# Fewer spent waits on TensorE in the second and third tile of a tiled recommender interaction

## The chip, the cores and the metric

The kernel runs on 1 core of one Trainium2 chip. The metric is the device time in microseconds (us). The kernel before was timed three times: 610.24, 610.33 and 610.54 us, median 610.33 us. In what follows an engine is named by its part in the profile: PE is TensorE's matrix product, PEld its loading of weights, DVE is VectorE, ACT is ScalarE, SP is SyncE.

## The reference, cut to what matters

```python
B, NF, D = 2048, 64, 128                    # r_F is (B, NF, D), all in float32
Kf  = einsum('bjd,ed->bje', F, K_w)         # keys: one 128x128 product per row of F
S   = einsum('bid,bjd->bij', F, Kf)         # a 64x64 score matrix per sample
out = einsum('bij,ijd->bid', S, W)          # each score row i times its own 64x128 matrix
out = out + einsum('bid,ed->bie', F, Q_w)   # plus a second 128x128 product of F
```

## The kernel before

The 2048 samples are cut into 16 tiles of 128 samples (`TILES`). A tile is 8 units of 16 samples, or 16 chunks of 512 columns (a chunk is 8 samples with their 64 features). For each tile TensorE runs three stages, called P, S and R here, with the tile's number behind:

- **P** (`project`, from line 472): for each of 16 chunks the product with the key matrix and the product with the query matrix. Each is done to nearly full float32 precision in three passes (`three`, line 446): high part by high part, high by low, low by high. That is 6 matrix instructions of 512 columns a chunk and 96 in a tile. ScalarE copies both results out of PSUM; ScalarE and VectorE split the coming units of F into a high and a low part.
- **S** (`scores`, line 500): 128 small float32 products, one for each sample; the profile has two records of 64 columns for each, so 256 in a tile. ScalarE and VectorE copy the scores to `s_t`.
- **R** (`rows_tile`, line 547): for every feature a product of 64 scores with its own matrix of W; 64 instructions, 128 records. VectorE adds the query part (`sum_out`, line 363) and SP stores 512 KB after each of 8 row blocks.

The order on TensorE is written out by hand at line 577: P0, then for each tile t: S(t), P(t+1), R(t). In the last tile two of the 16 query products are kept back and stand between S15 and R15 (`LATE = 2`, line 38), so P15 has 90 matrix instructions.

Every engine has its own list of instructions and waits on semaphores for the others. In `project` TensorE waits for the low half of the unit (`flo_done`, line 484), and for the PSUM bank it is about to write (`kf_copied`, line 487; `s_copied`, line 490; `q_copied`, line 493). Behind each chunk's two products the loop at lines 497 and 498 puts a number of waits on `zeros_done`. That semaphore is raised once, at the start of the kernel, so such a wait is always met: it is a spent wait, which does nothing but stand in TensorE's list of instructions. `FILL` (lines 41 to 43) says how many stand in a tile, spread evenly over the 16 chunks: 466 in tile 1, 108 in each of tiles 2 to 14, 128 in tile 15, none in tile 0. These are 1998 in all.

In the instructions that come of this, a wait that stands right ahead of a weight load rides on that load, and the others are packed two to one instruction. The profile shows them as event-semaphore instructions at the line of their first wait. By my count of the code a tile from 2 to 14 is 960 weight loads and matrix products and 64 such instructions, together 1024. P1 has 243 of them and a P of tiles 2 to 14 has 61, with the products' own waits and those behind the last chunk.

F comes in pairs of units, 1 MB each, into a ring of six places (`f_ring`). The first are loaded by SP at the start, with W (2 MB) behind them (line 181). The later ones are issued by ScalarE in `load_next` (line 244), one at the start of each P and one after its chunks 3, 7 and 11.

Of the kernel before, what the change touches and what calls it, by code (L numbers as in the profile page):

```python
# [14 lines left out]
TILES = B // P  # L15
# [22 lines left out]
LATE = 2  # L38


FILL = {1: 466}
FILL.update((t, 108) for t in range(2, TILES - 1))
FILL[TILES - 1] = 128

BOTH = [v for v in range(FIRST, TILES * UNITS) if v in (4, 5) or v >= UNITS and v % UNITS in (0, 4, 6)]

# [1 line left out]
def build(nc, first, f_0, f_t, w, out):  # L48
    with ExitStack() as ctx:  # L49
# [395 lines left out]
        def _(pe):  # L445
# [26 lines left out]
            def project(t):  # L472

                for c in range(CHUNKS):
# [21 lines left out]
                    if t >= 1:  # L496
                        for x in range(FILL[t] * c // CHUNKS, FILL[t] * (c + 1) // CHUNKS):
                            pe.wait_ge(zeros_done, 1)
# [110 lines left out]
```

## Time and profile before

| | |
|---|---|
| median of three runs | 610.33 us |
| the profiled execution | 610.46 us |
| its span, first to last instruction | 608.7 us |
| PE busy, share of the span | 599.6 us, 99% |
| ACT and DVE busy | 402.3 and 399.2 us, 66% each |
| DMA, mean over the span | 227 GB/s |

The span is the profiled execution without 1.8 us around it. A busy share is an average over stages of different kinds; the stages P, S and R have to be read by themselves. The profile's times are counted from the start of the span. A matrix product's record is longer than the distance to the next one, since the products overlap; distances between starts, and lengths of whole stages, are what time is made of.

### The profile page before, as it was taken

Reading aid. Unit: us, or ns where it says so; the run is one execution under the profiler, and the core shown is the slowest. Engines: PE = TensorE matmul, PEld = TensorE weight load, DVE = VectorE, ACT = ScalarE, POOL = GpSimd, SP = SyncE. Lnnn points to the kernel's source line nnn. Section 1 sums busy time; section 2 is a strip of 40 time slices with the busy share of each in tenths; the row PEclk is TensorE's granted clock in tenths of the full one; section 3 lists DMA queues with packets and bytes.
Section 4 is the critical chain, followed back from the end, with each engine's and each line's share of the span. In section 5 each row is a group of like instructions: output and inputs, shape, how many; then the busy total and the mean of one; then the engine's idle time right before and its main releaser. Section 6 shows DMA issues by size and latency. Waiting matters only on the chain.

```text
span 608.7 us, 18157 instructions
## 1 busy us (share of the span) xinstructions
PE 599.6 (99%) x7690; PEld 525.4 (86%) x7690; DVE 399.2 (66%) x412; ACT 402.3 (66%) x696; POOL 0.2 (0%) x4
## 2 busy tenths in 40 slices
PE   9999999999999999999999999999999999999995
PEld 7876988889898898988989888898988989889895
DVE  5644947658575676856759476585756768567386
ACT  7878295692938849386592956929488393865921
POOL 0000000000000000000000000000000000000000
PEclk9999999999999999999999999999999999999999
DMA  8633755647576485755657556475654857457177
GB/s 335 261 141 139 279 208 214 245 167 295 191 268 219 166 321 178 285 172 213 264 207 280 208 209 248 169 295 191 265 222 163 324 175 286 174 210 267 69 279 277
DMA packets 29453, 138.14 MB, mean 227 GB/s; under 512 B 3264, under 2 KB 3776, under 8 KB 21312
## 3 DMA queue, kind: packets, MB, share of 16 engines
q1 hardware_dynamic: 20736, 75.83, 31.6%
q10 hardware_dynamic: 8640, 61.15, 28.5%
q8 instruction: 64, 1.05, 0.7%
q14 instruction: 13, 0.11, 0.0%
HBM read 69.86 MB, written 67.11 MB: 225 GB/s over the span
## 4 chain that ended last, share of the span: by engine, by line
PE 97%; DVE 1%; issue 1%; DVEq 0%
PE ps L447 20%; PE ps L509 20%; PE ps L449 19%; PE ps L448 19%; PE ps L541 18%; DVE o_sb L372 1%; PE ps L576 1%; DVEq L49 0%; DVE o_sb L382 0%; PE ps L467 0%; PE ps L465 0%; PE ps L469 0%; DVE f_hi L388 0%; DVEq L115 0%
## 5 line engine op out<-in xcount | busy, mean ns | idle before, releaser
L337 DVE TENSOR_TENSOR f_lo<-f_ring,f_hi 128x1024 fp32r<-128x1024 f32 x124 | 151.8, 1224 | 169.5 <-ACT f_hi L217 167.9
L231 ACT ACTIVATE q_out<-ps 128x512 f32<-128x512 f32 x256 | 157.2, 614 | 6.9
L222 ACT ACTIVATE kf<-ps 128x512 f32<-128x512 f32 x256 | 155.9, 609 | 6.0 <-PE ps L449 2.2
L372 DVE TENSOR_TENSOR o_sb<-ps,q_out 128x1024 f32<-128x1024 f32 x127 | 145.1, 1214 | 20.1 <-PE ps L541 20.1
L240 ACT ACTIVATE s_t<-ps 128x512 f32<-128x512 f32 x32 | 19.1, 598 | 176.1 <-PE ps L509 176.1
L509 PE MATMUL ps<-f_ring,kf 128*64 128x64 f32 x4096 | 123.3, 222 | 0.3 <-issue 0.3
L509 PEld LDWEIGHTS ps<-f_ring,kf 128*64 128x64 f32 x4096 | 121.0, 138 | 2.6 <-issue 0.8
L541 PEld LDWEIGHTS ps<-s_t,w_sb 64*128 64x128 f32 x2048 | 115.6, 188 | 5.8 <-issue 5.8
L541 PE MATMUL ps<-s_t,w_sb 64*128 64x128 f32 x2048 | 118.6, 274 | 0.1
L447 PE MATMUL ps<-f_hi,k_hi 128*128 128x512 f32 x255 | 102.1, 400 | 0.6
L447 PE MATMUL ps<-f_hi,q_hi 128*128 128x512 f32 x256 | 99.9, 390 | 0.0
L449 PE MATMUL ps<-f_hi,q_lo 128*128 128x512 f32 x256 | 99.7, 390 | 0.0
L448 PE MATMUL ps<-f_lo,q_hi 128*128 128x512 f32 x256 | 99.6, 389 | 0.0
L449 PE MATMUL ps<-f_hi,k_lo 128*128 128x512 f32 x255 | 99.5, 390 | 0.0
L448 PE MATMUL ps<-f_lo,k_hi 128*128 128x512 f32 x255 | 99.4, 390 | 0.0
L217 ACT ACTIVATE f_hi<-f_ring 128x1024 fp32r<-128x1024 f32 x77 | 82.0, 1065 | 0.0
L447 PEld LDWEIGHTS ps<-f_hi,k_hi 128*128 128x128 f32 x255 | 47.8, 188 | 16.1 <-issue 6.0
L447 PEld LDWEIGHTS ps<-f_hi,q_hi 128*128 128x128 f32 x256 | 48.2, 188 | 10.2 <-ACT s_t L242 0.2
L448 PEld LDWEIGHTS ps<-f_lo,q_hi 128*128 128x128 f32 x256 | 48.1, 188 | 10.2
L449 PEld LDWEIGHTS ps<-f_hi,q_lo 128*128 128x128 f32 x256 | 48.0, 188 | 10.2
L449 PEld LDWEIGHTS ps<-f_hi,k_lo 128*128 128x128 f32 x255 | 47.9, 188 | 10.2
L448 PEld LDWEIGHTS ps<-f_lo,k_hi 128*128 128x128 f32 x255 | 47.9, 188 | 8.8
(39 smaller groups left out, 161.2 us busy)
## 6 DMA issues: line engine op xcount, KB each, us to landing
out<-o_sb SPq DMA_DIRECT2D x127, 512.0 KB, 3.4
f_ring<-f_t ACTq DMA_DIRECT2D x58, 1024.0 KB, 4.7
f_ring<-f_t SPq DMA_DIRECT2D x4, 1024.0 KB, 10.9
f_ring<-f SPq DMA_DIRECT2D x8, 256.0 KB, 5.7
w_sb<-w SPq DMA_DIRECT2D x1, 2048.0 KB, 18.2
out<-o_sb SPq DMA_DIRECT2D x2, 256.0 KB, 2.7
o_sb<-first SPq DMA_DIRECT2D x1, 192.0 KB, 2.9
o_sb<-first ACTq DMA_DIRECT2D x1, 192.0 KB, 3.4
```

The source lines that it names most:

```text
L217: nc.scalar.activation(f_hi[:, v % SPLIT, :], f_unit(v), COPY).then_inc(fhi_done, 1)
L222: nc.scalar.activation(kf[:, c // 2, c % 2 * CK:(c % 2 + 1) * CK, :, :].rearrange("d k h i -> d (k h i)"), ps[:, 2 * c % 8, :], COPY).then ...
L231: nc.scalar.activation(q_out[:, t % 2, :, :].rearrange("d i (h b) -> d i h b", h=2)[:, :, :, at:at + CK], q_bank(t * CHUNKS + c).rearrange ...
L240: nc.scalar.activation(s_t[:, :, same], src[:, 0, :, :], COPY)
L337: nc.vector.tensor_tensor(f_lo[:, v % SPLIT, :], f_unit(v), f_hi[:, v % SPLIT, :].bitcast(F32), ALU.subtract).then_inc(flo_done, 1)
L372: nc.vector.tensor_tensor(o_sb[:, n % OBUF, :, :, :].rearrange("d x s b -> d s x b"), ps[:, bank:bank + 2, :].rearrange("d s (x b) -> d s ...
L447: nc.tensor.matmul(dst, w_hi[:, :], hi, start=True, stop=False)
L448: nc.tensor.matmul(dst, w_hi[:, :], lo, start=False, stop=False)
L449: return nc.tensor.matmul(dst, w_lo[:, :], hi, start=False, stop=True)
L509: ins = nc.tensor.matmul(ps[h * N:(h + 1) * N, e, k * N:(k + 1) * N], kf[:, e, k, h, :], rows, start=True, stop=True)
L541: ins = nc.tensor.matmul(ps[:, at + s, col:col + P], w_sb[half, m, :], cols, start=True, stop=True)
L576: nc.tensor.matmul(ps[:, 0, :], zeros, zeros.unsqueeze(1).broadcast_to([D, BANK // P, P]), start=True, stop=True)
```

## The change

Three numbers: tile 1 gets no spent waits in place of 466, tile 2 gets 56 in place of 108, tile 15 gets 132 in place of 128. Tiles 3 to 14 keep 108. There are 1484 in all.

```diff
-FILL = {1: 466}
-FILL.update((t, 108) for t in range(2, TILES - 1))
-FILL[TILES - 1] = 128
+FILL = {1: 0, 2: 56}
+FILL.update((t, 108) for t in range(3, TILES - 1))
+FILL[TILES - 1] = 132
```

## Rows read from the trace of the kernel before

**Rows 1.** The page: busy time, share of the span, instructions.

```profile
span 608.7 us, 18157 instructions
...
PE 599.6 (99%) x7690; PEld 525.4 (86%) x7690; DVE 399.2 (66%) x412; ACT 402.3 (66%) x696; POOL 0.2 (0%) x4
```

**Rows 2.** The page: the chain that ended last, by engine.

```profile
PE 97%; DVE 1%; issue 1%; DVEq 0%
```

**Rows 3.** Table by stage: P1, P2, P3, P4, P15; window, length, busy, clock, DMA share, GB/s.

```profile
34.61:60.84 26.23, 25.50 (x100) 16.88 (x97) 10.98 (x11) 22.75 (x39) 0.00 (x0) 1.00 0.45 161
...
75.80:97.80 22.00, 22.00 (x100) 17.94 (x97) 10.99 (x11) 21.27 (x38) 0.00 (x0) 1.00 0.54 192
...
112.86:134.86 22.00, 22.00 (x100) 17.94 (x96) 10.90 (x11) 21.27 (x38) 0.00 (x0) 1.00 0.53 193
...
149.82:171.83 22.01, 22.01 (x101) 17.94 (x97) 11.00 (x11) 21.27 (x38) 0.00 (x0) 1.00 0.55 192
...
556.45:577.10 20.65, 20.65 (x94) 16.81 (x91) 8.06 (x8) 19.82 (x35) 0.00 (x0) 1.00 0.29 103
```

**Rows 4.** Line 498, spent waits alone: P1; 1.3 us within P1; P2.

```profile
L498 PEldq EVENT_SEMAPHORE  x212: 51/51/51, 34.6 to 60.4; - x106
...
L498 PEldq EVENT_SEMAPHORE  x12: 51/51/51, 35.7 to 36.9; - x12
...
L498 PEldq EVENT_SEMAPHORE  x32: 51/51/51, 76.8 to 93.8; - x32
```

**Rows 5.** Timeline of the weight loads, P1, around a chunk's start.

```profile
37.01 0.19 PEld L449 LDWEIGHTS ps<-f_hi,q_lo 128*128 128x128 f32 x1
37.38 0.19 PEld L447 LDWEIGHTS ps<-f_hi,k_hi 128*128 128x128 f32 x1 [0.18 <-issue]
```

**Rows 6.** Timeline of DVE: first splits of P1, then the same of P2.

```profile
39.59 1.22 DVE L337 TENSOR_TENSOR f_lo<-f_ring,f_hi 128x1024 fp32r<-128x1024 f32 x1 [4.63 <-ACT f_hi L217]
...
80.79 1.22 DVE L337 TENSOR_TENSOR f_lo<-f_ring,f_hi 128x1024 fp32r<-128x1024 f32 x1 [4.35 <-ACT f_hi L217]
```

**Rows 7.** Timeline of ACT's queue: loads of F in P1, then in P2.

```profile
34.74 0.33 ACTq L249 DMA_DIRECT2D f_ring<-f_t  x1
...
40.73 0.33 ACTq L249 DMA_DIRECT2D f_ring<-f_t  x1
...
75.93 0.33 ACTq L249 DMA_DIRECT2D f_ring<-f_t  x1
...
81.60 0.33 ACTq L249 DMA_DIRECT2D f_ring<-f_t  x1
```

**Rows 8.** SP's issue of W's load, and the page's time to landing.

```profile
7.98 0.43 SPq L181 DMA_DIRECT2D w_sb<-w  x1
```

```profile
w_sb<-w SPq DMA_DIRECT2D x1, 2048.0 KB, 18.2
```

**Rows 9.** Table by stage: S0, S1, S2, S4, S14, S15, and after S15.

```profile
26.99:34.61 7.62, 7.62 (x257) 7.55 (x257) 5.12 (x8) 3.61 (x6) 0.00 (x0) 1.00 0.02 4
...
68.18:75.80 7.62, 7.62 (x258) 7.55 (x257) 7.53 (x10) 1.78 (x3) 0.00 (x0) 1.00 0.88 339
...
105.14:112.86 7.72, 7.72 (x258) 7.63 (x257) 7.63 (x10) 1.78 (x3) 0.00 (x0) 1.00 0.86 332
...
142.21:149.82 7.61, 7.61 (x258) 7.54 (x256) 7.52 (x10) 1.78 (x3) 0.00 (x0) 1.00 0.87 339
...
548.84:556.45 7.61, 7.61 (x258) 7.54 (x256) 7.53 (x10) 1.78 (x3) 0.00 (x0) 1.00 0.87 336
...
584.44:592.71 8.27, 7.95 (x258) 7.67 (x256) 5.87 (x9) 3.56 (x6) 0.00 (x0) 1.00 0.80 312
592.71:608.67 15.96, 9.02 (x134) 8.27 (x134) 9.68 (x10) 2.25 (x5) 0.00 (x0) 0.93 0.67 264
```

**Rows 10.** Timeline of PE through S15: 147 records, a gap, 109 records.

```profile
584.45 4.53 PE L509 MATMUL ps<-f_ring,kf 128*64 128x64 f32 x147
589.27 3.42 PE L509 MATMUL ps<-f_ring,kf 128*64 128x64 f32 x109 [0.30 <-issue]
```

**Rows 11.** DMA queues: the whole span; 180.47 to 181.47 (S4); 586.75 to 587.75 (S15).

```profile
q8 instruction: 64, 1.05, 0.7%
...
q8 instruction: 1, 0.02, 8.0%
...
q8 instruction: 1, 0.02, 5.5%
```

## The prediction

> **What bounds the kernel now.** I read four views in this order. The page's busy times come first: PE is busy 99% of the span, and DVE and ACT 66% each [rows 1]. The chain of waits says the same from the other side: 97% of the chain that ended last is PE's own work [rows 2]. So time is won only where TensorE itself takes longer than its products need. The reader can't see that place in a busy share, since PE counts as busy nearly everywhere. It is seen in the third view, the table by stage [rows 3]. P2, P3 and P4 take 22.00, 22.00 and 22.01 us for 96 products, which is 0.2292 us each. P15, with 90 products, takes 20.65 us, or 0.2294 each. P1 has the same 96 products and takes 26.23 us. The clock granted is 1.00 in all five, so TensorE ran at the upper of its two levels and the clock does not explain the difference.
>
> What P1 has more of is the spent waits. The fourth view, the one of line 498, counts 212 wait instructions in P1 that hold nothing but spent waits, and 32 in P2 [rows 4]. Twelve of them in a row start between 35.7 and 36.9 us: 1.2 us over 11 steps, some 0.11 us each. With the products' own waits P1 has 243 wait instructions by the count of the code, P2 has 61.
>
> **Why 61 are free and 243 are not.** A chunk of P1 has six products and 243 / 16 = 15.2 wait instructions. The waits alone are about 15.2 x 0.11 = 1.7 us, and the six products need 6 x 0.2292 = 1.375 us. The measured chunk is 26.23 / 16 = 1.64 us. So in P1 the engine that hands out TensorE's instructions (the sequencer) is the bound: it spends its time on waits while the array runs dry, and the array gets the next chunk late. The weight load of each chunk's first product shows it, with 0.18 us of idle time put down to "issue" [rows 5]. In P2 a chunk has 3.8 wait instructions, some 0.4 us, which lie beside 1.375 us of products. That is the work which hides them, and it hides more of them the fewer there are.
>
> **The change part by part.**
>
> *Tile 1, 466 to 0.* 234 of P1's wait instructions go, 9 stay. The longest work left in a chunk is the six products. I take P2's length for P1: 26.23 - 22.00 = **-4.23 us**. The whole of it is on PE's chain, so it moves everything behind P1 forward.
>
> The question is what comes late next in a P1 that is 4.2 us shorter. VectorE: the first split of a new unit starts 39.59 - 34.61 = 4.98 us into P1, and 80.79 - 75.80 = 4.99 us into P2 [rows 6]. Both lie in the same place, so P1 can follow P2's schedule. ScalarE is busy 22.75 us in P1 and 21.27 us in P2 [rows 3]. This is tight (21.27 of 22.00), but P2 shows that it fits, with the same instructions. F: the first load is issued 0.13 us into both stages and the second 6.1 us into P1 and 5.8 us into P2 [rows 7]; it follows the chunks and will come earlier with them. W, which R0 waits for, was issued at 7.98 and landed 18.2 us later, at 26.2 us [rows 8]. R0 will begin at 60.84 - 4.23 = 56.6 us, so 30 us of cover stay. P1 has no stores beside it, which P2 does not have either (its stores end with S2's last part). The bounds for this part: nothing below 22.00 us is seen for 96 products, and if ScalarE's longer 22.75 us had to be fitted in, the stage would be 0.75 us longer. So -4.23 to -3.48, and I take -4.23 by the nearer row.
>
> *Tile 2, 108 to 56.* P2's wait instructions go from 61 to 41 by the count. All 61 were covered; taking 20 away gives 0. If the cover were gone, each would cost 0.11 us, so 20 of them would bring a gain of 2.2 us. But P2 has the same time per product as P15 with its 74 [rows 3], so the waits of P2 set nothing, and I leave this end out.
>
> *Tile 15, 128 to 132.* Four waits make one wait instruction more by the count, beside 1.375 us of products a chunk: 0 by itself.
>
> *Where the borders between instruction blocks come to lie.* The page shows 64 transfers of the instruction queue, 1.05 MB together, 16 KB each [rows 11]. TensorE's list is 16,550 instructions by the count, so one transfer is about 1.05 MB / 16,550 = 63 bytes times 256. Tiles 2 to 14 are 1024 instructions each, four blocks exactly, so the borders lie in the same places in each of them. S15 shows what one can cost: after 147 records PE stands, and the other 109 follow 0.3 us later by the records [rows 10]. The stage is 8.27 us instead of 7.61, a loss of 0.66. S2 is 7.72 us, a loss of 0.11; S1, S4 and S14 are 7.61 or 7.62, like S0 [rows 9]. In S4 the transfer lies 1.3 to 2.3 us into the stage, in S15 it lies 2.3 to 3.3 us into it [rows 11]. I read this as one block fetched late, because it stood behind the stores. The DMA engines are 80 to 88% busy in S1 to S15 [rows 9].
>
> The change takes 234 + 20 = 254 instructions out ahead of tile 3, two less than a block of 256. In rounds 3 to 14 each border thus lies 2 instructions earlier in its stage than now, which at S's pace (7.61 us / 512 instructions = 0.015 us) is 0.03 us. In S1 it lies 22 instructions earlier, 0.33 us: PE would reach the second border of S1 at about 4.07 us instead of 4.40. In S15 it lies 3 earlier. Bounds for all of it: from -0.77 (both present losses, 0.66 and 0.11, go) to +0.66 in each stage that is hit. I take 0, because 13 of the 15 stages with stores beside them lose nothing now (three of the 13 stand in [rows 9], and they are alike), and 0.03 us is little beside the 1 us by which the transfer was later in S15.
>
> **The sum.** 610.46 us in the profiled execution, less 4.23, is 606.23. That execution is 0.13 us over the median of the runs shown, 610.33, so a median run comes to **606.1 us**.
>
> A page of the Trainium skill speaks to the borders (Runtime: NRT & Kernel Launch, section Instruction fetch mechanics). It says that instructions come in 16 KiB blocks of 256, that the next is fetched while one runs, and that a crossing is mostly hidden. The trace agrees on the 16 KB and not on the hiding in S15. By that rule alone the borders would never cost and the sum would be the same less S15's and S2's losses, which is the second case below. Another page (Advanced Engine Details and Errata, section ISA Cache) gives that cache only two lines, so that a block must come within one block's running. That is the mechanism of the fourth case.
>
> **The rivals.**
>
> *The present losses vanish.* S15's border moves and the fetch falls better: 606.1 - 0.77 = **605.4**. For it: 13 of 15 stages are clean. Against: the median run is only 0.13 below the profiled one, so the runs without a profile seem to hold the loss too, and a border that moves 3 instructions changes little.
>
> *The unsettled rounds stall.* S1 has its border 0.33 us earlier and S2 is hit again: one or two stages at 0.66 each, 606.8 to **607.4**. For it: S2 already lost 0.11 with its present border. Against: S1 is the only stage with a real shift, and its fetch is asked for earlier too.
>
> *Slower: every round's second border in S is missed.* The block fetch has to fit between two borders of an S, 256 x 0.015 = 3.8 us, among stores. If the shift puts it behind one more store in each round, S1 to S14 lose up to 0.66 as S15 does now, 14 x 0.66 = 9.2, less S2's 0.11: 606.1 + 9.1 = **615.2**. It decides from 4.23 / 14 = 0.30 us lost in each round. For it: the fetch is late by only 1 us where it costs 0.66. Against: clean rounds with a shift of 0.03 us are expected to stay clean, since nothing else in them moves.
>
> *The waits are not what makes P1 long.* P1 is the first stage after the start; if its operands or ScalarE held it, nothing would be gained and the time stays at **610.3**. Against: the equal places of rows 6, and the idle time of rows 5, which is "issue" and no other engine.
>
> **How the numbers follow.** The forecast, 606.1, has 55%. Losses vanish: 20%. One or two new stalls: 17%. All rounds stall: 5%. No gain: 3%. What this kernel's measurement can tell from no change is about 0.2%, 1.2 us. The first three cases are all more than that below 610.33, so faster is 92%; no gain is same, 3%; and all rounds stalled is slower, 5%. The range takes the first case with P1's bound of 0.75 us, the second, and the third as far as one and a half stalls: 605.2 to 607.2. Left out are 8% for the last two cases and some of the third.
>
> **What would show it.** P1 would run from 34.6 to 56.6, 22.0 us long, and line 498 would have no instruction there; P1's weight loads would show no "issue" idle. P2 should stay at 22.00. The instruction queue should show 63 transfers instead of 64. S1 to S14 should be 7.61 to 7.62 each, with single ones up to 0.7 longer, and what lies behind S15 should stay at 15.96 us. The prediction is wrong if P1 stays over 22.8 us, or if most S stages are over 7.8 us, with a gap in PE's records after some 135 to 147 of the 256.

## The result, and the profile after

The changed kernel took 606.53 us (median of 6 runs, 605.90 to 607.51) against 610.29 us for the kernel before (6 runs, 609.90 to 610.54). The ratio is 0.994, with a 95% interval from 0.9929 to 0.9951. The forecast was 606.1 us, in a range of 605.2 to 607.2. The changed kernel's runs lie 1.6 us apart, where those of before lie 0.6 apart.

The profiled execution took 606.42 us with a span of 604.6. The table by stage is in the same columns as [rows 3] and [rows 9]. The stages are P1, P2, S2, S3, S6, S14, P15, S15 and what lies behind S15:

```profile
34.45:56.43 21.98, 21.98 (x100) 17.94 (x96) 10.69 (x11) 21.25 (x38) 0.00 (x0) 1.00 0.55 193
...
71.39:93.63 22.24, 22.24 (x100) 17.87 (x96) 11.00 (x11) 21.42 (x38) 0.00 (x0) 1.00 0.54 190
100.98:109.13 8.15, 7.88 (x258) 7.67 (x257) 7.84 (x10) 1.78 (x3) 0.00 (x0) 1.00 0.81 317
...
138.46:146.24 7.78, 7.78 (x258) 7.67 (x256) 7.69 (x10) 1.78 (x3) 0.00 (x0) 1.00 0.85 331
249.50:257.25 7.75, 7.75 (x258) 7.67 (x256) 7.66 (x10) 1.78 (x3) 0.00 (x0) 1.00 0.86 331
545.37:552.99 7.62, 7.62 (x259) 7.55 (x257) 7.53 (x10) 1.78 (x3) 0.00 (x0) 1.00 0.87 337
552.99:573.63 20.64, 20.64 (x94) 16.81 (x90) 8.06 (x8) 19.82 (x35) 0.00 (x0) 1.00 0.29 103
580.98:588.70 7.72, 7.68 (x258) 7.54 (x257) 5.87 (x9) 3.56 (x6) 0.00 (x0) 1.00 0.86 334
588.70:604.60 15.90, 9.02 (x134) 8.27 (x134) 9.67 (x10) 2.25 (x5) 0.00 (x0) 0.92 0.67 266
```

P1 is 21.98 us long in place of 26.23. ScalarE, which stood at 22.75 us there, is now at 21.25. No wait instruction of line 498 is left in P1; the first one in the span starts at 70.9 us:

```profile
L498 PEldq EVENT_SEMAPHORE  x498: 51/51/51, 70.9 to 570.9; - x166
```

The weight load that opens a chunk of P1 no longer has idle time before it (in [rows 5] it had 0.18 us), and the instruction queue has 63 transfers:

```profile
36.85 0.19 PEld L449 LDWEIGHTS ps<-f_hi,q_lo 128*128 128x128 f32 x1
37.08 0.19 PEld L447 LDWEIGHTS ps<-f_hi,k_hi 128*128 128x128 f32 x1
```

```profile
q8 instruction: 63, 1.03, 0.7%
```

So much is as forecast. The S stages are not all clean. A clean one takes 7.61 or 7.62 us; S2 took 8.15, S3 7.78 and S6 7.75. P2 took 22.24 us, with the extra time behind its 7th product. S1, whose border moved most, is clean:

```profile
63.78:71.39 7.61, 7.61 (x258) 7.54 (x256) 7.52 (x10) 1.78 (x3) 0.00 (x0) 1.00 0.88 341
```

S15, at 7.72 us, is clean too. PE's records in it show no gap. The 0.11 us over 7.61 stand at its end, where the weight load of the first kept-back query product waits for ScalarE's copy of the scores:

```profile
588.70 0.19 PEld L447 LDWEIGHTS ps<-f_hi,q_hi 128*128 128x128 f32 x1 [0.17 <-ACT s_t L242]
```

The kernel before has the same wait there:

```profile
592.71 0.19 PEld L447 LDWEIGHTS ps<-f_hi,q_hi 128*128 128x128 f32 x1 [0.16 <-ACT s_t L242]
```

So of the 0.66 us that [rows 9] show for S15 over a clean stage only 0.55 are the late block.

The timeline of PE through S2 shows the same picture as [rows 10], one record earlier, after 146:

```profile
100.98 4.53 PE L509 MATMUL ps<-f_ring,kf 128*64 128x64 f32 x146
105.78 3.42 PE L509 MATMUL ps<-f_ring,kf 128*64 128x64 f32 x110 [0.27 <-issue]
```

The account between the two spans (608.7 to 604.6, -4.1 us): S0 begins 0.16 earlier (26.83 for 26.99), P1 -4.25, P2 +0.24, the late blocks in S from 0.66 (S2 0.11, S15 0.55) to 0.85 (S2 0.54, S3 0.17, S6 0.14), +0.19, the end behind S15 -0.06. That is -4.04; the rest is rounding and a few hundredths in other P stages. The present loss of S15 went, and three new ones came.

### The profile page after: what moved, and what is told of

Read it like the earlier page. It is cut to its first block, busy times and chain, and to the rows that moved or that the text cites. A ratio compares the mean times of both kernels' runs of the same rounds, so it can differ in the third digit from the quotient of the medians.

```text
span 604.6 us, 17904 instructions
## 1 busy us (share of the span) xinstructions
PE 596.4 (99%) x7690; PEld 526.3 (87%) x7690; DVE 399.2 (66%) x412; ACT 401.5 (66%) x696; POOL 0.2 (0%) x4
## 4 chain that ended last, share of the span: by engine, by line
PE 98%; DVE 1%; issue 1%; DVEq 0%
PE ps L509 20%; PE ps L447 20%; PE ps L449 19%; PE ps L448 19%; PE ps L541 18%; DVE o_sb L372 1%; PE ps L576 1%; DVEq L49 0%; DVE o_sb L382 0%; PE ps L467 0%; PE ps L465 0%; PE ps L469 0%; DVE f_hi L388 0%; DVEq L115 0%
```

## The experiments

In all of them a place x means: the first border between two blocks of 256 instructions lies x instructions into S (and into P and R, where the tile is 1024 instructions), by the count of the code. The kernel before has x = 40 in S1 to S14 and 39 in S15. The changed kernel has 18 in S1, 38 in S2 to S14 and 36 in S15. The count rests on one shift, taken from the gap of [rows 10]; every gap that follows is a test of it. The loss shows at the second border, 256 instructions behind the first. By the formula a gap should stand after (256 + x) / 2 - 1 records of S, give or take one.

**Twice the waits of tile 1.** The kernel before with

```diff
-FILL = {1: 466}
+FILL = {1: 978}
```

> The kernel before with 978 spent waits in tile 1 in place of 466, 256 wait instructions more by the count, so every border behind P1 lies where it lay before. Theory A (sequencer bound, each wait instruction some 0.106 us): 256 x 0.106 = 27.1 us more, 637.4 us, P1 53.3 us. Rival B (P1 was long for another reason, such as operands that come late after the start): about 610.3 us, no more than 2 us above.

It took 638.09 us (638.02 to 638.18), ratio 1.045 (1.0436 to 1.0463). P1 and P2 by stage:

```profile
34.48:88.49 54.01, 26.00 (x101) 16.80 (x97) 11.01 (x11) 25.50 (x40) 0.00 (x0) 1.00 0.23 78
103.45:125.43 21.98, 21.98 (x101) 17.94 (x97) 10.99 (x11) 21.25 (x38) 0.00 (x0) 1.00 0.55 192
```

Line 498 alone has 468 instructions in P1 here, against 212 in [rows 4], so the 256 more that the count gave are there. P1 grew by 54.01 - 26.23 = 27.78 us for them: 0.1085 us each. That times 243 is 26.4 us, and the P1 of before is 26.23. So P1's length was set by the number of its wait instructions, and theory A stands.

**As many waits as before, spread over two tiles.**

```diff
-FILL = {1: 466}
-FILL.update((t, 108) for t in range(2, TILES - 1))
+FILL = {1: 233, 2: 341}
+FILL.update((t, 108) for t in range(3, TILES - 1))
```

> About as many wait instructions as before, spread over two tiles: 233 spent waits in tile 1, 341 in tile 2, the rest as before (the borders from S2 on lie 38 instructions into a stage, as in the changed kernel from S2 on). Theory A (waits are free below some 13 wait instructions a chunk, since 13 x 0.106 = 1.375 us of products): P1 22.0 us, P2 22.0 us, total about 606.5 us, plus up to 0.7 for S1, whose borders lie 157 instructions in. Rival B (every spent wait costs, or the number of instructions does): 610.3 us, as before.

It took 607.36 us (606.91 to 607.71), ratio 0.9946 (0.9934 to 0.9958). P1 and P2, and the instructions of line 498 in each:

```profile
34.40:56.39 21.99, 21.99 (x101) 17.95 (x97) 10.70 (x11) 21.25 (x38) 0.00 (x0) 1.00 0.54 192
71.82:93.81 21.99, 21.99 (x99) 17.95 (x97) 11.49 (x12) 21.26 (x38) 0.00 (x0) 1.00 0.55 192
```

```profile
L498 PEldq EVENT_SEMAPHORE  x95: 51/51/51, 34.4 to 52.9; - x95
...
L498 PEldq EVENT_SEMAPHORE  x150: 51/51/51, 71.8 to 91.0; - x150
```

P2 holds 150 instructions of pure spent waits and is as fast as P1 with 95 or the changed kernel's with none. As many waits as before cost nothing when spread thinly enough; only their density in P1 of before did. Rival B falls. The median lies 0.8 us over the changed kernel's: in the profile S1, with x = 157, took 8.09 us, with its gap after 206 records where the formula asks for it, and S15 took 8.31.

**The part for tile 1 alone.** Tiles 2 and 15 keep 108 and 128; x is then 18 in every round.

```diff
-FILL = {1: 466}
+FILL = {1: 0}
```

> The part for tile 1 alone: 466 to 0, tile 2 keeps 108, tile 15 keeps 128. Theory A (P1 was bound by the handing out of its waits; a border's place matters): P1 is 22.0 us as in the changed kernel, but the borders now stay 18 instructions into every stage, where P2 of the changed kernel lost 0.24 us. If each of P2 to P15 loses 0.24, the time is 606.5 + 13 x 0.24 = 609.6 us. Rival B (the place of the borders does not matter, only the waits of tile 1 do): 606.5 us, as the whole change. Between 607.3 and 608.8 neither holds as stated.

It took 614.16 us (609.90 to 616.27, 12 runs), ratio 1.0048 (1.003 to 1.0067): half a per cent slower than the kernel before. Both theories missed, A by its price and its place. P1 has its 22 us, but the S stages have lost more than P1 won. S1, P2, S2, S5 and S9 by stage:

```profile
64.07:72.53 8.46, 7.83 (x258) 7.67 (x256) 7.83 (x10) 1.78 (x3) 0.00 (x0) 1.00 0.79 306
72.53:94.52 21.99, 21.99 (x99) 17.94 (x96) 10.69 (x11) 21.26 (x38) 0.00 (x0) 1.00 0.54 192
101.87:110.35 8.48, 7.83 (x259) 7.68 (x257) 7.84 (x10) 1.78 (x3) 0.00 (x0) 1.00 0.78 304
215.35:223.83 8.48, 7.83 (x259) 7.67 (x257) 7.84 (x10) 1.78 (x3) 0.00 (x0) 1.00 0.78 304
...
365.41:373.02 7.61, 7.61 (x258) 7.54 (x257) 7.52 (x10) 1.78 (x3) 0.00 (x0) 1.00 0.87 339
```

Nine S stages took 8.46 to 8.48 us, one took 7.97 and three 7.69; S9 took 7.61, and S15 7.72 without a gap. The loss of S1 to S14 together is 8.4 us, against 0.1 in the kernel before. The gap in S2 stands after 136 records, as x = 18 asks:

```profile
101.87 4.19 PE L509 MATMUL ps<-f_ring,kf 128*64 128x64 f32 x136
106.70 3.72 PE L509 MATMUL ps<-f_ring,kf 128*64 128x64 f32 x120 [0.65 <-issue]
```

The DMA queues tell S2 (late) from S9 (clean). The first row is S2 from 2.3 to 3.3 us into the stage, the second S9 from 1.4 to 2.4 us into it. Each holds the start of the block's transfer; S2 has none in the window of 1.0 to 2.0 us:

```profile
q8 instruction: 1, 0.02, 5.8%
...
q8 instruction: 1, 0.02, 6.0%
```

**No spent waits at all.** A tile is 972 instructions, and x is another in each round.

```diff
-FILL = {1: 466}
-FILL.update((t, 108) for t in range(2, TILES - 1))
-FILL[TILES - 1] = 128
+FILL = {t: 0 for t in range(1, TILES)}
```

> No spent waits in any tile. A tile is then 972 instructions, so the borders lie in another place in each round (18, 70, 122, 174, 226, 22, 74, ... instructions into S). Theory A (a border in a bad place stalls PE, and the waits are there to keep it out of there): some rounds lose 0.2 to 1 us in S, P or R; I expect 3 to 8 us in all, 609 to 614 us. Rival B (the spent waits of tiles 2 to 15 do nothing): 606.0 to 606.5 us, as the changed kernel.

It took 614.64 us (613.43 to 615.89), ratio 1.0064 (1.005 to 1.0077). S2 (x = 70), S3 (122), S5 (226) and S11 (26):

```profile
101.08:109.38 8.30, 7.88 (x259) 7.67 (x257) 7.84 (x10) 1.78 (x3) 0.00 (x0) 1.00 0.80 310
138.75:146.99 8.24, 7.84 (x259) 7.68 (x257) 7.84 (x10) 1.78 (x3) 0.00 (x0) 1.00 0.81 317
213.59:221.41 7.82, 7.82 (x258) 7.67 (x256) 7.62 (x10) 1.78 (x3) 0.00 (x0) 1.00 0.84 330
438.96:446.58 7.62, 7.62 (x259) 7.55 (x257) 7.53 (x10) 1.78 (x3) 0.00 (x0) 1.00 0.87 338
```

14 of the 15 S stages with stores beside them run over 7.62 us; S11 alone is clean. The place decides in part where the transfer falls: PE passes the first border of S3 at 122 x 0.01487 = 1.8 us and the transfer starts at 3.7, in S5 it is 3.4 and 5.0. In every S1 to S15 traced, the block that PE needs at the second border is sent only after PE has passed the first. The spent waits of tiles 2 to 15 do nothing by themselves and are worth some 8 us here, by where they put the borders. Rival B falls.

**Three more places.** The changed kernel with another number in tile 2, which sets x from S2 on. 80 spent waits there give x = 30, 32 give 54, and none give 70. The first of the three edits:

```diff
-FILL = {1: 0, 2: 56}
+FILL = {1: 0, 2: 80}
```

> The changed kernel with 80 spent waits in tile 2 in place of 56: from S3 on (by the count from S2 on) the borders lie 30 instructions into a stage, not 38. Theory A (the border's place sets how often the second block of S comes late): between the 614.2 us of 18 instructions and the 606.5 us of 38; with the share of stages hit falling evenly, 609.5 us. Rival B (only the one place of 18 is bad, through P): 606.5 us.

> The changed kernel with 32 spent waits in tile 2: borders 54 instructions into a stage from S2 on. Theory A1 (later is better, since 18 is worst and 38 and 40 good): 606.0 us or less. Theory A2 (there is a best place near 40, and beyond it the fetch falls among the stores again, as the round of 70 in the kernel without spent waits lost 0.69): 608 to 612 us. Rival B (place does not matter beyond 38): 606.5 us.

> The changed kernel with no spent waits in tile 2 either: borders 70 instructions into a stage from S2 on. In the kernel without any spent waits the single rounds with 70, 74 and 78 lost 0.69, 0.63 and 0.30 us in S. Theory A2: each of S2 to S15 loses about 0.5 us, 606.5 + 14 x 0.5 = 613 us. Rival B or A1: 606.5 us or less.

They took 613.02 us (ratio 1.0047, 1.0034 to 1.006), 613.71 us (1.0049, 1.0034 to 1.0064) and 615.15 us (1.0074, 1.0062 to 1.0086). Theory A2 holds: there is a narrow good place near 40, with slow ones on both sides. All three missed their expectation in size. For x = 30 the fall was expected to be even (609.5 us), and it is a step: 30 is nearly as bad as 18. For x = 54, 608 to 612 us were expected. For x = 70 a loss of 0.5 us a stage was expected (613 us), and it was 0.4 to 0.7, mostly 0.63. One S3 of each, in the order 30, 54, 70:

```profile
139.26:147.55 8.29, 7.88 (x258) 7.67 (x257) 7.85 (x10) 1.78 (x3) 0.00 (x0) 1.00 0.80 311
```

```profile
138.10:146.55 8.45, 7.88 (x258) 7.67 (x256) 7.84 (x10) 1.78 (x3) 0.00 (x0) 1.00 0.79 305
```

```profile
138.87:147.10 8.23, 7.88 (x259) 7.67 (x257) 7.84 (x10) 1.78 (x3) 0.00 (x0) 1.00 0.81 314
```

The gap of x = 70 stands after 162 records, again where it should:

```profile
138.87 5.00 PE L509 MATMUL ps<-f_ring,kf 128*64 128x64 f32 x162
144.21 2.96 PE L509 MATMUL ps<-f_ring,kf 128*64 128x64 f32 x94 [0.35 <-issue]
```

With the transfers' times the loss follows one sum, as an estimate. PE gets to the second border at (256 + x) x 0.01487 us into S (7.61 us / 512 instructions); the block is taken to be of use 1.57 us behind the end of its transfer. All times are counted from the start of S:

| kernel, stage | x | transfer starts, ends | PE at the border | sum | measured loss |
|---|---|---|---|---|---|
| tile 1 alone, S2 | 18 | 2.41, 3.34 | 4.07 | 0.84 | 0.87 |
| x = 30, S4 | 30 | 2.42, 3.35 | 4.25 | 0.67 | 0.67 |
| changed, S2 | 38 | 2.41, 3.34 | 4.37 | 0.54 | 0.54 |
| x = 54, S7 | 54 | 2.74, 3.70 | 4.61 | 0.66 | 0.53 |
| x = 54, S4 | 54 | 2.40, 3.34 | 4.61 | 0.30 | 0.29 |
| x = 70, S4 | 70 | 3.00, 3.88 | 4.85 | 0.60 | 0.63 |
| before, S4 | 40 | 1.43, 2.71 | 4.40 | below 0 | 0 |

The 1.57 is fitted to these rows, and it serves all but one of them to 0.03 us. Over all stages S1 to S14 of the traces with full stores it serves the 31 whose transfer starts at 2.4 to 2.5 us (places 18 to 54) to 0.06 us; elsewhere the sum is off by up to 0.2 us (S7 of tile 1 alone: sum 0.30, measured 0.08). So it orders the stages and is no exact law.

What separates good from bad is in the main the start of the transfer. It is not fixed by x: it comes at 1.3 to 2.1 us or at 2.4 us and later, and x sets how often. These are all stages S1 to S14 with full stores at these six places, from the traces of all kernels together:

| x | stages | transfer starts at 2.3 us or later | mean loss |
|---|---|---|---|
| 18 | 22 | 11 | 0.46 |
| 30 | 13 | 9 | 0.47 |
| 38 | 52 | 3 | 0.05 |
| 40 | 55 | 1 | 0.01 |
| 54 | 13 | 13 | 0.44 |
| 70 | 14 | 14 | 0.62 |

S1 is the plainest case. The changed kernel, the one with tile 1's part alone and those with x = 30, 54 and 70 hold the same instructions on TensorE up to S1, where x is 18 in all of them. In the profiles S1 was clean with the changed kernel and with x = 54, and took 8.46 to 8.48 us with the other three.

**Half of the stores' bytes.** The kernel with tile 1's part alone (x = 18), which stores the first half of each row block and leaves the other half of the output out, but for the first block of the last tile:

```diff
-                sp.dma_start(out[t, k, :, :],
-                             o_sb[:, n % OBUF, :, :, :].rearrange("d x s b -> d (x s b)"))...
+                sp.dma_start(out[t, k, :, 0:IR * P],
+                             o_sb[:, n % OBUF, 0:IR // 2, :, :].rearrange("d x s b -> d (x s b)"))...
```

> The kernel with borders 18 instructions in (tile 1 without spent waits, the rest as before) stores only the first half of each row block's results, 256 KB in place of 512, but for the first block of the last tile; the other half of the output is left out. Theory A (the block of instructions comes late since its transfer stands among the stores): the 0.87 us losses in S go, all S stages 7.6 us, 605.5 to 606.5 us in place of 614.2. Rival C (the loss at a border in S comes from the pace of the sequencer itself, whatever the DMA engines do): 614 us, as with full stores.

It took 603.95 us (603.87 to 604.35). S2, S3, and what lies behind S15:

```profile
101.06:108.72 7.66, 7.66 (x258) 7.59 (x256) 7.57 (x10) 1.78 (x3) 0.00 (x0) 1.00 0.39 143
138.05:145.71 7.66, 7.66 (x259) 7.59 (x257) 7.57 (x10) 1.78 (x3) 0.00 (x0) 1.00 0.39 143
...
588.20:602.60 14.40, 9.01 (x134) 8.27 (x134) 9.70 (x10) 2.24 (x5) 0.00 (x0) 0.91 0.45 166
```

The DMA engines' share in S2 falls from 0.78 to 0.39, and the loss of S1 to S14 together from 8.4 to 0.5 us, with the borders at the same x = 18. The block's transfer starts at 1.64 us into S at the latest. What lies behind S15 is some 1.5 us shorter, which accounts for a time under the expected 605.5; the last stores are half as long there, which is the likely reason. Rival C falls: the stores are what makes the block late.

**Tile 15's part, 40 for 38, and an earlier settling.** Four kernels on one chip. The first puts the wait instructions of before where they are covered, in tiles 0 and 1, so that x = 40 from S1 on and 36 in S15:

```diff
-FILL = {1: 0, 2: 56}
-FILL.update((t, 108) for t in range(3, TILES - 1))
-FILL[TILES - 1] = 132
+FILL = {0: 120, 1: 350}
+FILL.update((t, 108) for t in range(2, TILES - 1))
+FILL[TILES - 1] = 134
...
-                    if t >= 1:
+                    if t >= 0:
```

> The 234 wait instructions that moved the borders to 40 are kept, but none of them where it can be seen: 120 spent waits in tile 0, 350 in tile 1 (some 12 wait instructions a chunk), 108 in tiles 2 to 14, 134 in tile 15. By the count the borders lie 40 instructions in from S1 on, and 36 in S15. Theory A: P1 22.0 us, and the losses of the changed kernel in P2, S2 and S3 (0.24, 0.54 and 0.17 us) go, 605.4 to 605.9 us, faster than the changed kernel by 0.5 to 1.1. Rival (12 wait instructions a chunk are too many, or tile 0 is held by its waits): P1 at 23 us or more, or S0 begins later than 26.8 to 27.1 us, and the time is 606.5 us or more.

The second is the changed kernel with `FILL[TILES - 1] = 128`:

> The changed kernel with 128 spent waits in tile 15, as before; the border in S15 then lies 38 instructions in by the count, not 36. If tile 15's part of the change matters, S15 loses 0.65 us as it did before and in the spread version, and the time is 607.0 us. If it is chance, S15 loses about as often as other stages, and the time is 606.5 us.

The third is the changed kernel with `2: 58`:

> The changed kernel with 58 spent waits in tile 2 in place of 56: borders 40 instructions in from S2 on, not 38. Theory A (the stages lose at 38 a little more often than at 40; the kernel before lost nothing in 13 stages at 40): 0.2 to 0.5 us faster than the changed kernel, 606.0 to 606.3 us. Rival (38 and 40 are alike): 606.5 us.

The fourth is the changed kernel once more:

> The changed kernel once more, on the chip of the other three, to compare them with: 606.5 us, P1 22.0 us, one to four S stages with a loss between 0.1 and 0.6 us.

| kernel | median | lowest, highest | ratio to before |
|---|---|---|---|
| early settling | 605.95 | 605.55, 606.76 | 0.9922 (0.9905 to 0.9938) |
| tile 15 with 128 | 606.81 | 606.04, 607.35 | 0.9934 (0.9917 to 0.995) |
| x = 40 from S2 on | 606.17 | 605.99, 606.39 | 0.9924 (0.9908 to 0.994) |
| changed kernel again | 607.18 | 606.22, 607.96 | 0.9942 (0.9924 to 0.9961) |

Tile 15's part shows no effect: 606.81 us lies between the two expected values and under the changed kernel's 607.18. With 128 its S15 took 8.33 us. The changed kernel with 132 had 7.72 the first time and 8.31 now, so that clean S15 was the exception: in seven of the eight profiles with x = 36 to 40 there, S15 took 8.26 to 8.33.

```profile
580.79:589.12 8.33, 8.01 (x258) 7.73 (x256) 5.88 (x9) 3.56 (x6) 0.00 (x0) 1.00 0.80 310
```

```profile
580.10:588.41 8.31, 7.95 (x259) 7.73 (x257) 5.87 (x9) 3.56 (x6) 0.00 (x0) 1.00 0.80 310
```

The changed kernel again was expected at 606.5 us and took 607.18; in its profile only S14 (7.78) and S15 lost. x = 40 is better than 38: all six of its runs lie under five of the changed kernel's six on this chip, and no S stage but S15 lost anything in its profile. In the four profiled kernels with 38 from S2 on, S2 to S14 lost 0.84, 1.01, 0.67 and 0.17 us together, in the four with 40 they lost 0.10, 0.10, 0.08 and nothing. The two quicker kernels are the best of those that store all of the output. Settling already in S1 brought no more than chance over x = 40 (0.2 us between medians, runs overlapping). Its profiled execution, 606.76 us, was the slowest of its six runs and lost 0.49 us in S1. Its median, 605.95, lies just outside the expected 605.4 to 605.9 and 1.2 under the changed kernel's, where 0.5 to 1.1 was expected; how much S1 has to do with it stays open. P1 was 21.99 us long there with 154 instructions of pure spent waits, so the rival of too many waits falls.

## Why the prediction was right

- *What P1's length was made of.* Right, and shown: 0.1085 us per wait instruction by doubling them, and no cost at all with up to 154 in a stage of 22 us. Forecast -4.23 us, measured -4.25.
- *What would be late next in P1.* Nothing was: 21.98 us, ScalarE at 21.25. The upper bound of 0.75 us for ScalarE was not needed.
- *Tile 2, 108 to 56.* "Taking 20 away gives 0" is right for the waits as such. But this part of the change is what puts the borders at 38. Without it they stay at x = 18, and the kernel takes 614.2 us in place of 606.5: the part is worth 7.6 us, more than P1's. The prediction counted the 20 in for the borders and gave them no price.
- *Where the borders come to lie.* Right that the loss is a block fetched late among the stores, and that the shift matters. The term was mis-sized at 0. The medians moved by -3.76 us where -4.23 was forecast, and by -3.43 (610.61 to 607.18) on the second chip, so the borders of the changed kernel, with P2's 0.24 in some executions, cost 0.5 to 0.8 us more than those of before. The reason given, that 0.03 us is little beside 1 us, was weak: the slack of a clean stage is far less than 1 us. In the kernel before, a transfer that ended 2.82 us into S was free, and one that ended at 3.01 cost 0.10; the clean ones end at 2.3 to 2.8, so the slack is 0.5 us at most and nothing in some. The price of a late block, 0.66, was read 0.11 us too high, since S15's own wait at its end was counted with it.
- *Luck.* The forecast's 0 came near because x = 38 lies in the good place. That place is less than 24 instructions wide (30 and 54 are bad), and the prediction did not ask how wide. The change was laid out to move the borders by 2 only, which is no luck; that 2 would do no harm was not known.
- *The unsettled rounds.* S1 was expected to stall with 17%, for its real shift of 22 instructions. It was clean in both profiles of the changed kernel, which was chance too: at x = 18 half of the stages traced have a late transfer. S2, the other stage of this case, was hit in one of the two profiles (0.54), and the second median, 607.18, lies in this case's span of 606.8 to 607.4.
- *The slower rival.* "Every round's second border in S is missed" is real. It was priced at 615.2 us with 5%; the kernels at x = 18, 30, 54 and 70 measured 613.0 to 615.2. What kept the change out of it is the one number in tile 2.
- *Losses vanish.* This case would have been 605.3 (606.1 - 0.77), not 605.4. S15's loss did vanish in the profiled execution, but as an exception, and S2's grew to 0.54.
- *The stores beside P1 and P2.* The prediction says that they end with S2's last part. It is S1's: the stores' queue has 86.5% of the DMA engines' time over S1 of the kernel before and 0.5% over the first 4.2 us of P2. Nothing hangs on it.
- *The rule on hidden crossings.* The Trainium skill (Runtime: NRT & Kernel Launch, section Instruction fetch mechanics) says that crossing a border between blocks is mostly hidden. That holds here wherever the DMA engines have room: every R stage is clean (DMA share 0.56 to 0.57), nearly every P (0.54), and S with half the stores (0.39) loses 0.05 us or less. With the share at 0.86 to 0.88, as at x = 40, it still holds in most stages; at x = 54 and 70 it fails in all of them.

**What stays open.** Why the transfer starts at 1.4 us in nearly all stages at x = 38 and 40 but at 2.4 us in half or more of those at 18 and 30, where it should be asked for earlier, is not shown. The moment of the stores does not tell them apart: in the kernel with tile 1's part alone they are issued 1.49 and 0.36 us before S and 0.77 and 1.90 us into it, in the late S2 and in the clean S9 alike. Whether the transfer meets one of them in a queue wasn't tried. Nor is it shown what makes single executions lose in S2, or why S15 loses in nearly all of them.

## What to carry to other kernels

On TensorE an instruction that holds only waits which are already met (up to two of them) took about 0.11 us here. It was free while the products beside it took longer: 154 in a stage of 22 us cost nothing, 243 made it 26 us. So count wait instructions per product, not in all. In a long unrolled stream, look where the borders between blocks of 256 instructions fall in the stage with the shortest instructions and the fullest DMA engines. A few instructions more or less early on move all of them, and here that won or lost more than what the change was made for. To test a place, move the borders with spent waits in a stage that has cover, and read after how many records PE stands still.

## What was not expected of the hardware

- A block's arrival decides within a few hundredths of a us: x = 40 against 38 is 0.03 us in S, and 0.4 to 1.0 us in the kernel's median (606.17 against 606.53 and 607.18).
- The same instructions at the same place can have their block in time or not: at x = 18 the transfer started at 1.4 to 1.6 us in half of the stages traced and at 2.4 in the other half. Where it starts at 2.4 the loss goes by PE's own arrival, 0.015 us an instruction (0.87, 0.67, 0.54 us at 18, 30, 38).
- Taking 466 spent waits out of tile 1 made the kernel slower (614.16 against 610.53 us) when nothing else was changed.
